# Moving one group's choice, ranks, slots and run lists from the last token tiles into the first early tiles

## What is computed

```python
# x: (64, 64, 1024); W = cond_weights[itok]: (64, 64, 64)
y = jnp.einsum('bct,bcd->bdt', x, W)
logits = y @ W_gate + b_gate                       # 8 experts
_, top_idx = jax.lax.top_k(logits, 2)
y_all = jax.nn.relu(jnp.einsum('bsd,edh->bseh', y, W_e) + b_e)
out = x + jnp.take_along_axis(y_all, top_idx[..., None], axis=2).mean(axis=2)
```

## Time and profile before

| | us |
|---|---|
| median of 3 runs | 888.14 |
| lowest, highest | 887.94, 890.49 |
| the profiled execution | 888.81 |
| its span | 887.1 |
| TensorE busy in it | 851.0 |
| VectorE busy | 428.5 |
| GpSimd busy | 446.5 |
| ScalarE busy | 256.9 |

### The profile page before, as it was taken

How to read it: one execution, slowest core, us unless ns; L and a number is a source line. 1 busy time by engine, 2 the same in 40 slices (tenths; PEclk the granted TensorE clock), 3 DMA queues, 4 the chain that set the end, 5 groups by cost and what they waited for, 6 DMA issues and landing times.

```text
span 887.1 us, 16691 instructions
## 1 busy us (share of the span) xinstructions
PE 851.0 (96%) x4154; PEld 674.1 (76%) x4155; DVE 428.5 (48%) x578; ACT 256.9 (29%) x310; POOL 446.5 (50%) x500
## 2 busy tenths in 40 slices
PE   7788899999999999999999999999999999999993
PEld 4344468888888888888888888888888888888883
DVE  6698876847643373335533373336433733333320
ACT  5555412134522252114311331115111511111220
POOL 3002224366566647654665556555655565555411
PEclk9899999999999999999999999999999999999997
DMA  9999698998965686547754594547664655444433
GB/s 335 418 415 351 227 330 265 341 333 251 288 158 109 130 266 136 106 95 196 200 103 93 98 298 101 107 100 213 171 118 95 189 114 109 91 101 97 82 48 47
DMA packets 51034, 162.47 MB, mean 183 GB/s; under 512 B 11594, under 2 KB 11658, under 8 KB 50986
## 3 DMA queue, kind: packets, MB, share of 16 engines
q0 software_dynamic: 24544, 76.74, 40.4%
q1 hardware_dynamic: 20618, 67.79, 21.0%
q10 hardware_dynamic: 5840, 17.57, 5.0%
HBM read 106.74 MB, written 70.52 MB: 200 GB/s over the span
## 4 chain that ended last, share of the span: by engine, by line
PE 88%; DVE 6%; DMA 2%; issue 2%; ACT 1%; ACTq 0%; POOL 0%; DVEq 0%; POOLq 0%
PE psO L606 85%; DVE turned L855 2%; PE psO L547 2%; DMA y_rows<-ys 1%; ACT ys L699 1%; DMA raw<-in_L_cond_weights 1%; DVE w_lo L868 1%; PE psG L559 0%; DVE run_hot L918 0%; DVE place_hot L910 0%; DVE idx_all L884 0%; DVE idx_all L883 0%; DVE idx_all L886 0%; DVE raw L885 0%; PE psL L571 0%
## 5 line engine op out<-in xcount | busy, mean ns | idle before, releaser
L606 PE MATMUL psO<-w_hi,a_hi 128*128 (+1 forms) x1104 | 341.7, 391 | 0.3 <-issue 0.3
L606 PE MATMUL psO<-w_lo,a_hi 128*128 (+1 forms) x1104 | 340.6, 390 | 0.0
L606 PE MATMUL psO<-w_hi,a_lo 128*128 (+1 forms) x1104 | 340.4, 390 | 0.0
L464 POOL DMA_INDIRECT rows<-y_rows,idx_g x248 | 255.7, 1031 | 106.8 <-issue 52.1
L606 PEld LDWEIGHTS psO<-w_hi,a_lo 128*128 128x128 f32 x1104 | 207.5, 188 | 43.4
L606 PEld LDWEIGHTS psO<-w_lo,a_hi 128*128 128x128 f32 x1104 | 207.6, 188 | 43.3
L606 PEld LDWEIGHTS psO<-w_hi,a_hi 128*128 128x128 f32 x1104 | 206.9, 188 | 44.1 <-issue 1.7
L1031 DVE TENSOR_TENSOR a_lo<-ys,a_hi 128x1024 fp32r<-128x1024 f32 x62 | 75.9, 1224 | 115.6 <-ACT a_hi L735 115.6
L723 ACT ACTIVATE ys<-ys 128x1024 f32<-128x1024 f32 x33 | 35.0, 1061 | 258.1 <-DVE ys L993 258.1
L723 ACT ACTIVATE rows<-rows 128x1024 f32<-128x1024 f32 x33 | 35.0, 1061 | 252.7 <-DVE rows L993 252.7
L993 DVE TENSOR_TENSOR ys<-psO,bias 128x1024 f32<-128x1024 f32 x33 | 40.2, 1219 | 124.6 <-PE psO L606 108.3
(11 more groups left out here) (141 smaller groups left out, 337.4 us busy)
## 6 DMA issues: line engine op xcount, KB each, us to landing
raw<-in_L_ffn_W_e SPq DMA_DIRECT2D x56, 512.0 KB, 6.2
y_rows<-ys ACTq DMA_DIRECT2D x32, 512.0 KB, 8.3
out<-in_x SPq DMA_DIRECT2D x14, 1024.0 KB, 9.3
rows<-in_x SPq DMA_DIRECT2D x16, 512.0 KB, 10.1
more_x<-in_x SPq DMA_DIRECT2D x16, 512.0 KB, 11.0
bias<-in_L_ffn_b_e SPq DMA_DIRECT2D x8, 512.0 KB
rows<-y_rows,idx_g POOLq DMA_INDIRECT x248
raw<-in_L_ffn_W_e POOLq DMA_DIRECT2D x4, 512.0 KB, 9.0
```

The costliest lines, as they stand in the source:

```text
L464: pool.indirect_dma_start(out=rows[:, slot, a * DQ:(a + 1) * DQ], out_offset=None, in_=y_parts[0:(1 + TOK) * Q, :], in_offset=bass.Indirec ...
L606: last = nc.tensor.matmul(ps[:, h * BANK:(h + 1) * BANK], a[:, p, k * P:(k + 1) * P], w[:, bass.ds(slot + (k * H + h * BANK), BANK)], star ...
```

## The change

A constant `LATE` = 5 is added. Choice, ranks, slots and run lists of groups 0 to 4 stay where they were; those of group 5 leave the last token tiles. `unstack(5)` stays at token tile 27, and `unstack(6)`, at tile 31 before, becomes a hook. The hooks of groups 5 to 7 are laid out anew over early tiles 0 to 2, VectorE's steps behind the loop are put in a new order, and SyncE loads the first bias and reads early tile 4's slots ahead of the first copies.

```diff
-        UNSTACK = {G * g + 7: g for g in range(NG - 1)}
-        RANKS = {G * g + 9: g for g in range(NG - 2)}
-        FILL = {G * g + 11: g for g in range(NG - 2)}
-        LIST = {G * g + 12: g for g in range(NG - 3)}
+        UNSTACK = {G * g + 7: g for g in range(LATE + 1)}
+        CHOOSE = {G * g + 7: g for g in range(LATE)}
+        RANKS = {G * g + 9: g for g in range(LATE)}
+        FILL = {G * g + 11: g for g in range(LATE)}
+        LIST = {G * g + 12: g for g in range(LATE)}
...
+                sp.wait_ge(s_split, KD)
+                load_bias(0)
+                read_first(4)
                 sp.wait_ge(s_y, NTILE - 2)
                 copy(0)
                 copy(1)
 
                 sp.dma_start(out[TOK:TOK + P, :], x_rows[0:P, :]).then_inc(s_pad, 16)
-                sp.wait_ge(s_split, KD)
-                load_bias(0)
-                table_out(NG - 3)
-                read_first(4)
+                table_out(LATE)
                 copy(2)
                 copy(3)
-                table_out(NG - 2)
                 read_first(5)
+                table_out(LATE + 1)
                 copy(4)
                 copy(5)
-                table_out(NG - 1)
                 read_first(6)
+                table_out(LATE + 2)
                 for c in range(6, len(left)):
                     copy(c)
...
-                early_products(0, hooks={3: lambda: ranks(NG - 2), 4: lambda: gate(NG - 1, 1, 0),
-                                         5: lambda: gate(NG - 1, 1, 1), 7: lambda: unstack(NG - 1)})
-                early_products(1, hooks={0: lambda: fill(NG - 2), 2: lambda: ranks(NG - 1), 7: lambda: fill(NG - 1)})
-                early_products(2)
+                early_products(0, hooks={1: lambda: gate(NG - 1, 1, 0), 2: lambda: gate(NG - 1, 1, 1),
+                                         3: lambda: ranks(NG - 3), 5: lambda: unstack(NG - 2), 7: lambda: fill(NG - 3)})
+                early_products(1, hooks={2: lambda: ranks(NG - 2), 4: lambda: unstack(NG - 1), 6: lambda: fill(NG - 2)})
+                early_products(2, hooks={1: lambda: ranks(NG - 1), 6: lambda: fill(NG - 1)})
...
-                    if n in UNSTACK:
-                        choose(UNSTACK[n])
+                    if n in CHOOSE:
+                        choose(CHOOSE[n])
...
+                choose(NG - 3)
+                turn_early(1)
+                slots(NG - 3)
+                early_lo(1)
+                choose(NG - 2)
                 list_out(NG - 3)
+                finish_early(0)
+                early_out(0, 4)
+                turn_early(2)
                 slots(NG - 2)
-                turn_early(1)
-                early_lo(1)
+                early_lo(2)
                 choose(NG - 1)
                 list_out(NG - 2)
-                finish_early(0)
+                read_from(4)
+                finish_early(1)
+                turn_early(3)
                 slots(NG - 1)
-                read_from(4)
-                turn_early(2)
-                early_lo(2)
+                early_lo(3)
                 list_out(NG - 1)
-                finish_early(1)
-                early_out(0, 4)
                 read_from(5)
-                turn_early(3)
-                early_lo(3)
                 turn_early(4)
                 finish_early(2)
                 early_lo(4)
```

More of the change, by code:

```diff
@@ L44, in build @@
     FIRST = 3
+    LATE = 5
     TPE = TOK // P
```

## The result

| | before, us | after, us |
|---|---|---|
| median (runs) | 888.64 (18) | 892.78 (18) |
| lowest, highest | 886.31, 892.30 | 890.59, 895.32 |
| the profiled execution | 888.81 | 895.25 |
| its span | 887.1 | 893.6 |

The ratio is 1.0044, with a 95% interval of 1.0032 to 1.0055: the change makes the kernel slower, by 4.1 us in the medians. The profiled execution of after lies at the upper end of its runs and is 6.4 us over that of before. First the page of after, as the earlier trace rows: busy times, then the shares of the chain that ended last, by engine and by line.

What follows compares the result with a forecast made beforehand. TensorE is 96% busy, VectorE sets the pace before 115 us, DMA engines bound from 142 us to expert 1's weights. Profiled 888.81 + 3.5 (tile 8) + 1.64 (clock) = 893.95, or 893.3 against the median; range 887.0 to 897.5.

Steps and rivals of the forecast that it cites:

- The front: Up to tile 7: expert products start 5.2 us earlier; after hook and clock terms TensorE leads by 4.5 us.
- Lists and SyncE: SyncE's queue: later lists delay table writes and the copies behind them, so expert 1's weights arrive 1.1 us later.
- POOL's transfers: DMA engines: gathers and scatters issued earlier put 2.4 us more work ahead of expert 1's weights.
- Tile 8: Ninth tile: starts at 212.7 instead of 209.21; TensorE waits 8.3 us, losing all the lead and 3.5 us more.
- Clock: Behind the pause at tile 8: the granted clock falls to half, costing 1.6 us.
- Behind tile 8: Products after tile 8 run without pause: no time given back, and nothing added for tile 12.
- the signs named: Changed kernel's profile: L606 near 110, pause near 204 then clock 0.50, copies from about 152, weights from 185 or later.
- The scatter of early tile 4: POOL's queue: a sign that this scatter, at 198.44 before, would be issued before the last `w_hi`.
- the lead reaches the end: Rival, whole kernel: the 4.5 us lead is kept past tile 8, giving 883.6 us; chance 0.10.
- The weights stand still: Rival, at tile 8: weights come no later, tile 8 starts at 209 to 210, giving 888.1 to 890.8; chance 0.23.

Runs made afterwards that it cites:

- experiment 1: After, with copies 6 to 13 from `x` to `out` cut to their first 64 of 1024 columns: 884.07 us, ratio 0.9935.
- experiment 2: Before, with copies 6 to 13 from `x` to `out` cut to their first 64 of 1024 columns: 888.22 us, ratio 0.9988.
- experiment 4: After, with expert 1's bias and first four weight blocks issued ahead of copies 10 to 13: 885.54 us, ratio 0.9957.
- experiment 5: Before, with expert 1's first four weight blocks issued ahead of copies 10 to 13: 888.28 us, ratio 0.9990.
- experiment 11: After itself, unchanged, measured again on a second chip as a control: 895.03 us, ratio 1.0049.
- experiment 3: After, with 32 products whose result nobody reads put between tile 7 and tile 8: 891.22 us, ratio 1.0026.
- experiment 6: After, with copies 2 to 7 moved, a pair at a time, ahead of a table write: 893.52 us, ratio 1.0044.

## Why the prediction was right, point by point

The forecast was 893.3 us with a range of 887.0 to 897.5; the median is 892.78. The mechanism is the forecast one, a lead that is lost at tile 8 to weights queued behind the copies, and experiments 1, 2, 4 and 5 show it. Its terms, in the prediction's order:

- **The front.** Forecast: a lead of 4.5 us, tile 7 done at 204.4, the first hook waiting 1.1 us, the full clock kept. Measured: 4.6, 204.3, 1.09, and a clock of 1.00. Experiments 1 and 2 confirm it by the end of the kernel (4.2 us). All rows for it stood in the trace of before. One was misread: the slots of group 5 end at 114.46 and not at 114.97, where the next transpose starts; no term uses it.
- **Lists and SyncE, +1.1 us.** Measured +1.8. The pair of copies that opens the full stretch was forecast at 142.2 and came at 144.02, because the table write ahead of it began 0.5 us later than forecast and took 4.94 us, where that at 143.77 before took 3.56. The pair is 4.15 us later than before, yet the eight copies start only 1.81 us later. The size was off; the cause is as forecast, by these rows.
- **POOL's transfers, +2.4 us.** This was the mis-sized term. Between the weights' issue and the last `w_hi` there are only 2.62 - 1.82 = 0.8 us more, whatever their cause. The step that failed: I let VectorE and POOL follow TensorE's lead. They did not. POOL turns to the gather of tile 7 at 174.00 and did at 174.99 before, and the scatter of early tile 4, forecast near 192, is at 198.04 in after and was at 198.44 before:

```profile
156.37 0.23 DVE L975 TENSOR_SCALAR from_q<-first,part_q 128x4 uint32<-128x4 uint32 x1 [3.95 <-DMA first<-slot_table]
...
167.07 1.61 POOL L484 DMA_INDIRECT out<-more_x,first_to  x1 [3.61 <-DMA out<-in_x]
174.00 0.31 POOL L463 COPY idx_g<-idx_all 128x4 uint32 x1 [5.32 <-issue]
...
198.04 1.61 POOL L484 DMA_INDIRECT out<-rows,first_to  x1 [3.91 <-issue]
```

  These are VectorE's row and three of POOL's. VectorE waits 3.95 us for the slots of early tile 6, read behind two copies; it is at that row at 156.37, where it was at 156.94 before, so its lead of 4.6 us is down to 0.6. The index tables, which POOL's gather of tile 7 needs, come behind it. The scatter at 167.07 waits for copies, but that is not what holds the gather: in experiment 1 this scatter goes out at 163.75, and the gather still at 174.01. From there to the scatter of early tile 4 POOL loses 0.6 us more, and what holds it there is open.
- **Tile 8.** Forecast 212.7, a wait of 8.3 us, 8.4 us from the last `w_hi`. Measured 211.84, 7.52 and 8.39. The loss is 2.63 us instead of 3.5.
- **Clock, +1.6 us.** Measured 2.92 in the profiled execution. I took eight products at half speed from the pause before 115 us; here twelve records were at half speed, 211.84 to 217.13 = 5.29 us instead of 12 x 0.2269 = 2.72, 2.6 us of the 2.9. In experiment 11 tile 8 lost only 2.2. The step that failed was to take the price of one pause, 8 products, for that of another.
- **Behind tile 8.** I added nothing. 0.9 us appeared at tile 11 (0.73 in experiment 11), and it goes when the clock stays up (experiment 3).

So the sum came out near because errors offset: 0.9 too much at tile 8, 1.3 and 0.9 too little behind it. In the profiled execution it was forecast as +5.1 and is +6.4, while in the medians it is +4.1; the forecast lies between the two. It was also made from a median of before of 888.14, which with more runs is 888.64: of the forecast step of +5.2 us in the medians, 4.1 came. That 893.3 and 892.78 lie 0.5 us apart is in good part luck.

Of the signs named, those for the front, the pause and its clock, the copies (152.17) and the weights (185.28) came. The scatter of early tile 4 ahead of the last `w_hi` came too, but it was so in before (198.44 and 200.83) and tells nothing.

Of the rivals, "the lead reaches the end" (883.6) named the right condition: the last `w_hi` 4.5 us earlier. Experiment 4 meets it (the split of the first four blocks begins at 187.88) and comes to 885.5, 1.9 us above that rival; its waits at tiles 9 and 12 are 2.5 us. Experiment 1 meets it too (192.13) and comes to 884.07. "The weights stand still" fell with the 1.8 us in SyncE's queue.

## What to carry to other kernels

A pause of 0.28 us can hide a second bound that is level with the first: before speeding up one engine, ask of each short pause what the other chain would do if the engine came early, and move that chain in the same change. A queue that mixes small reads on the critical chain with large copies should be ordered by when each is needed: here four weight blocks ahead of four copies turned +4.1 us into -3.3 us. After each wait removed the next stood close behind (1.7 us at tile 9, then up to 3.7 at tile 12), so here no shift paid its full size.

## What the runs showed of the hardware

- Four small reads of slots, issued just behind two copies of 1 MB in the same queue, took 9.2 to 9.9 us to land in after; behind a table write they took 4.6 to 6.3 in before. In experiment 6 a table write of eight small transfers behind two copies, issued by 148.85, let the read that needs it go at 155.81.
- A wait of 7.5 us in mid-kernel cost 2.9 us more in the half clock that followed, in the profiled execution of after, and one of 8.2 us cost 2.2 in that of experiment 11. The same wait filled with idle products did not lower the clock (1.00 in every window from 204 to 220 in experiment 3), but the timed medians did not follow: -1.6 us with 32 products, none with 24.
- Two executions of the same kernel were at the half clock for 10.2 and 6.8 us, 4.6 and 2.9 of them still in the pauses of 7.52 and 8.16 us: the longer pause had the shorter stretch.
